# Sort pass of a graph network: VectorE's comparisons read the row of numbers from a PSUM bank

## The reference

```python
h = jnp.maximum(_layernorm(x, axis=-1), 0.0)
# layer 0, with row = src, col = dst
x_j = node_features[col]
m = jnp.einsum('ei,ej,ijh->eh', x_j, edge_attr_e3nn, W_msg_tp) * norm_msg_tp
m = jax.nn.silu(m)
m = m @ W_msg_lin * norm_lin
agg = jax.ops.segment_sum(m, row, num_segments=n_nodes)
...
x = x + layer0; x = x + layer1; x = x + layer2; x = x + layer3
```

## Time and profile before

| | |
|---|---|
| time, median of three runs | 19862.05 us (19857.42 to 19865.26) |
| the profiled execution | 19815.21 us, span 19813.6 us |
| instructions | 553,798 |
| PE busy over the whole span | 15287.0 us (77%) |
| DVE busy over the whole span | 13621.7 us (69%) |
| POOL busy over the whole span | 5755.4 us (29%) |
| stretch of the sort pass's scatters | 417.7 to 5958.6 us |

### The profile page before, as it was taken

How to read it: one execution, slowest core, us unless ns; L and a number is a source line. 1 busy time by engine, 2 the same in 40 slices (tenths; PEclk the granted TensorE clock), 3 DMA queues, 4 the chain that set the end, 5 groups by cost and what they waited for, 6 DMA issues and landing times. The chain is left out here.

```text
span 19813.6 us, 553798 instructions
## 1 busy us (share of the span) xinstructions
PE 15287.0 (77%) x200647; PEld 13589.7 (69%) x201524; DVE 13621.7 (69%) x32754; ACT 8118.3 (41%) x17256; POOL 5755.4 (29%) x4543
## 2 busy tenths in 40 slices
PE   2666666666666997799999999997688888856665
PEld 1666666666664996688888888886566666646565
DVE  3777777777775997555555555554677777769899
ACT  0444444444442332355555555553344444421111
POOL 1888888888880110011111111110000000001111
PEclk9555555555555997899999999998899999977676
DMA  2222222222222553344444444443344444427676
GB/s 56 54 54 50 53 54 54 54 52 52 54 51 66 157 157 91 91 110 110 110 110 108 112 109 111 108 111 80 114 139 139 140 142 139 139 61 210 173 209 181
DMA packets 1402755, 2062.56 MB, mean 104 GB/s; under 512 B 764952, under 2 KB 938022, under 8 KB 1359282
## 3 DMA queue, kind: packets, MB, share of 16 engines
q1 hardware_dynamic: 1089098, 1709.41, 27.8%
q0 software_dynamic: 218240, 197.29, 9.1%
q10 hardware_dynamic: 94544, 142.53, 2.0%
HBM read 1521.71 MB, written 523.16 MB: 103 GB/s over the span
## 5 line engine op out<-in xcount | busy, mean ns | idle before, releaser
L759 POOL DMA_INDIRECT records<-e_sort_rec,e_sort_index x3300 | 4328.5, 1312 | 1063.8 <-issue 989.5
L2442 POOL DMA_DIRECT2D states<-e_s_second_t x550 | 475.4, 864 | 4685.2 <-ACT e_s_second_t L2139 4342.2
L1088 PE MATMUL e_sort_acc<-e_sort_thirds,e_sort_hot 128*128 128x48 f32 x7260 | 1574.6, 414 | 320.8 <-DVE e_sort_hot L918 320.8
L1088 PEld LDWEIGHTS e_sort_acc<-e_sort_thirds,e_sort_hot 128*128 128x128 f32 x7260 | 1556.9, 332 | 353.2 <-DVE e_sort_hot L918 353.2
L2284 PE MATMUL e_s_ps_g<-e_s_parts,e_s_pick 128*128 128x64 bf16 x32670 | 1419.9, 198 | 276.0 <-DVE e_s_g_sb L1943 256.0
L2433 POOL DMA_INDIRECT e_s_spill<-send,e_s_lists x220 | 299.9, 1363 | 4257.3 <-PE e_s_ps_h L2344 3214.0
L2284 PEld LDWEIGHTS e_s_ps_g<-e_s_parts,e_s_pick 128*128 128x128 bf16 x32670 | 1301.5, 101 | 339.2 <-DVE e_s_g_sb L1943 290.8
L1943 DVE COPY e_s_g_sb<-e_s_ps_g 128x512 f32<-128x512 f32 x440 | 303.5, 690 | 1483.6 <-PE e_s_ps_h L2303 1376.5
L1926 DVE TENSOR_SCALAR e_s_pick<-e_s_rows,lane_below 128x1024 bf16<-128x1024 bf16 (+1 forms) x3300 | 1247.5, 436 | 3.2 <-PE e_s_ps_h L2326 3.1
L1005 ACT ACTIVATE e_sort_away<-iota,e_sort_slots 128x128 f32<-128x128 f32 x3850 | 1171.0, 388 | 10.7
L2354 PEld LDWEIGHTS e_s_ps_o<-w_eblk,e_s_act 128*128 128x128 f32 x7920 | 1040.8, 192 | 169.8 <-issue 146.5
(11 more groups left out here) (548 smaller groups left out, 37148.2 us busy)
## 6 DMA issues: line engine op xcount, KB each, us to landing
e_s_rows<-rows_d SPq DMA_DIRECT2D x330, 1088.0 KB, 5.3
e_s_hot<-hots_d SPq DMA_DIRECT2D x550, 560.0 KB, 3.9
e_s_to_rows<-rows_d SPq DMA_DIRECT2D x220, 608.0 KB, 5.4
e_s_rows<-rows_d SPq DMA_DIRECT2D x220, 544.0 KB, 4.1
e_s_rows<-rows_d SPq DMA_DIRECT2D x220, 512.0 KB
e_s_to_rows<-rows_d SPq DMA_DIRECT2D x220, 512.0 KB
states<-e_s_first_t ACTq DMA_DIRECT2D x440, 256.0 KB
states<-e_s_second_t POOLq DMA_DIRECT2D x440, 256.0 KB
```

The costliest lines, as they stand in the source:

```text
L759: pool.indirect_dma_start(records, bass.IndirectOffsetOnAxis(ap=index[x][:, t:t + 1], axis=0), rec[x][:, t, :], None,).then_inc(written[x] ...
L1088: mm = pe.matmul(acc[c // ACC][:, c % ACC * SPAN * F:(c % ACC + 1) * SPAN * F], hot[:, c, :], thirds[:, c, :, :].rearrange("p h f -> p (h ...
```

## The change

The row of numbers is also copied into PSUM, into columns 256 to 383 of `acc[3]` (`ps_iota`), once, after TensorE has blanked the four sum banks. The running sums are laid out anew: cells 0, 1 and 2 move into `acc[3]`, and the other thirty into `acc[0]` to `acc[2]`, ten each. The comparisons L818 and L823 and groups 0, 2 and 3 of L918 read the numbers from PSUM; group 1 of L918 goes on reading them from SBUF. TensorE signals a new step `early` when it has added cell 2, the last one that goes into `acc[3]`. VectorE waits for it ahead of group 2 of L918, and, for the block summed last, ahead of L818. In between, while group 1 is compared, TensorE may write `acc[3]`. The four final copies on ScalarE follow the new layout.

```diff
-            bt = Chain(sem(f"{name}_sum_t"), 0, ["rows"] + [f"added{g}" for g in range(len(HOTS))] + ["merged"])
+            bt = Chain(sem(f"{name}_sum_t"), 0, ["rows", "early"] + [f"added{g}" for g in range(len(HOTS))] + ["merged"])
...
+            ps_iota = acc[3][:, 256:256 + LANES]
+            blanked, iota_placed = sem(f"{name}_blanked"), sem(f"{name}_iota_placed")
+
+            def sum_bank(c):
+                return 3 if c < 3 else (c - 3) // ACC
+
+            def sum_at(c):
+                first = c if c < 3 else (c - 3) % ACC
+                return slice(first * SPAN * F, (first + 1) * SPAN * F)
...
                     dve.wait_ge(av.sem, av.at("cell", k))
+                    if before >= 4:
+                        dve.wait_ge(bt.sem, bt.at("early", k - 4))
                     dve.tensor_tensor(hot_c[:, :, :], bc3(cell[:, :], [P, BLOCK_T, SPILL]),
-                                      iota128[0:P, 0:SPILL].unsqueeze(1).broadcast_to([P, BLOCK_T, SPILL]), ALU.is_equal).then_inc(av.sem, 1)
+                                      ps_iota[0:P, 0:SPILL].unsqueeze(1).broadcast_to([P, BLOCK_T, SPILL]), ALU.is_equal).then_inc(av.sem, 1)
...
                         dve.tensor_tensor(hot_d[:, t:e, :], bc3(dlo[x][:, t:e], [P, e - t, LANES]),
-                                          iota128[0:P, :].unsqueeze(1).broadcast_to([P, e - t, LANES]), ALU.is_equal).then_inc(av.sem, 1)
+                                          ps_iota[0:P, :].unsqueeze(1).broadcast_to([P, e - t, LANES]), ALU.is_equal).then_inc(av.sem, 1)
...
                     for g, (c, e) in enumerate(HOTS):
+                        numbers = iota128[:, :] if g == 1 else ps_iota
+                        if g == 2:
+                            dve.wait_ge(bt.sem, bt.at("early", k))
                         dve.tensor_tensor(hot[:, c:e, :], bc3(lower[:, c:e], [LANES, e - c, LANES]),
-                                          iota128[:, :].unsqueeze(1).broadcast_to([LANES, e - c, LANES]), ALU.is_equal).then_inc(bv.sem, 1)
+                                          numbers.unsqueeze(1).broadcast_to([LANES, e - c, LANES]), ALU.is_equal).then_inc(bv.sem, 1)
...
                 dve.wait_ge(flushed, 7)
+                dve.wait_ge(blanked, 1)
+                dve.tensor_copy(ps_iota, iota128[:, :]).then_inc(iota_placed, 1)
+                dve.wait_ge(iota_placed, 1)
...
-                            mm = pe.matmul(acc[c // ACC][:, c % ACC * SPAN * F:(c % ACC + 1) * SPAN * F], hot[:, c, :],
+                            mm = pe.matmul(acc[sum_bank(c)][:, sum_at(c)], hot[:, c, :],
                                            thirds[:, c, :, :].rearrange("p h f -> p (h f)"), start=False,
-                                           stop=last and (c % ACC == ACC - 1 or c == OWN - 1), skip_group_check=True)
+                                           stop=last and (c == 2 or c % ACC == 2 and c > 2), skip_group_check=True)
+                            if c == 2:
+                                mm.then_inc(bt.sem, 1)
                         mm.then_inc(bt.sem, 1)
```

More of the change, by code:

```diff
@@ L1028, in _ @@
                 act.wait_ge(bt.sem, bt.end(BLOCKS - 1))
-                for b in range(4):
-                    act.activation(total[:, b * ACC * SPAN * F:min(CHUNKS, (b + 1) * ACC * SPAN) * F],
-                                   acc[b][:, 0:(min(CHUNKS, (b + 1) * ACC * SPAN) - b * ACC * SPAN) * F], ACT.Copy).then_inc(sums_flushed, 1)
+                for c in (0, 3, 3 + ACC, 3 + 2 * ACC):
+                    n = 3 if c == 0 else ACC
+                    act.activation(total[:, c * SPAN * F:(c + n) * SPAN * F], acc[sum_bank(c)][:, 0:n * SPAN * F], ACT.Copy).then_inc(sums_flushed, 1)
                 act.wait_ge(sums_flushed, 4)
@@ L1099, in _ @@
                 for b in range(4):
-                    pe.matmul(acc[b][:, :], blank[:, 0:LANES], blank[:, :], start=True, stop=False, skip_group_check=True)
+                    mm = pe.matmul(acc[b][:, :], blank[:, 0:LANES], blank[:, :], start=True, stop=False, skip_group_check=True)
+                mm.then_inc(blanked, 1)
                 def body(k, x, before):
```

## The result

The changed kernel took 19584.62 us in the median of 4 runs (19566.84 to 19610.17), the kernel before 19863.65 (19857.42 to 19886.99; three of its four runs are those of the table above): ratio 0.986, 95% interval 0.9845 to 0.9875. That is 279 us less, over four times the 64 that were forecast, and outside the range. The same two programs, run again in later batches, gave 0.9869 in one and 1.0008 in another. A batch is here a set of kernels run one after another on one chip, with the kernel before among them.

A forecast was written before the change was run, and what follows sets the result against it. POOL's scatters bound the kernel at 50.44 us a block, with TensorE's loop about 1 us shorter. 0.48 us x 108 = 52 us plus 12 us of lead make 64: 19862 - 64 = 19798 us, range 19700 to 19865.

The forecast's parts named there:

- The stretching: POOL's scatters L759, lengthened by VectorE comparisons with two SBUF operands: 2.46 us a block less, minus 0.5 kept by group 1.
- POOL's period, forecast at 48.5: POOL's time per block would fall by 1.96 us from 50.44 to 48.5 us; bounds of the fall 1.3 and 2.5.
- VectorE and the new wait: VectorE comparisons take no longer from PSUM; waiting for early before group 2 of L918 lasts 0.2 to 0.5 us, cost zero.
- The 65 ns: Skill-based estimate of extra time per VectorE instruction reading PSUM; would add 7 us in TensorE's loop; left out of the sum.
- That TensorE's loop becomes the bound: The loop of TensorE, ScalarE and VectorE, 49.5 us in the block shown, limits the block once POOL gets shorter.
- The sign that the prediction gave for being wrong: POOL's scatters still follow without a wait and the pass ends 200 us earlier; then TensorE's loop was elastic.
- What TensorE's loop gives back: Only its waits for VectorE's place stage: 0.24 us a block at L1044, 0.24 at L1067 (bounds 0 and 0.70); 52 us.
- The base of the sum: Period of 50.44 us a block before, falling to 49.96; the gain is taken off the median of 19862 us.
- POOL keeps the bound: Rival: TensorE's loop can follow down to 48.5 us, so all 1.96 us a block come off: 19646 us; chance 0.12.
- TensorE's loop is the bound already: Rival: the 0.48 us reappear as waits elsewhere in the loop; 19830 to 19862, say 19848 us; chance 0.20.
- the one slower case that I gave: Rival: TensorE's gathers L1067 lose their fast clock, 4.4 us in a block that loses it; 19919 us; chance 0.08.
- The lead of 12 us: Message values (L987) are ready 13 us before POOL takes them; this shrinks to nothing, so the last block starts 12 us earlier.

The follow-up runs named there:

- fourth batch: Changed kernel again 0.9869; kernel before with 14 of 30 scatters 0.9815; changed kernel with all four sum-stage comparison groups from PSUM 0.9841.
- third batch: Same programs again: kernel before 1.0004, changed kernel 1.0008, changed kernel with 28 of 30 scatters 0.9976, kernel before with 28 scatters 0.9949.
- a_place: Changed kernel, but the four sum-stage comparisons (L918) read the numbers from SBUF again, only the place stage from PSUM: 19740 us (0.9937).
- a_sum: Changed kernel, but the place-stage comparisons (L818, L823) read from SBUF again, without their wait; three sum-stage groups from PSUM: 19761 us (0.9946).
- b28: Kernel before with 28 instead of 30 scatters per block, two record columns left out: 19783 us (0.9944), again 19761 us (0.9949).
- Batches 1, 3 and 5: Batch 1: kernel before with 28 scatters 0.9944, with sorted records loaded a body later 0.9979; changed kernel with 28 scatters 0.9956, 32 scatters 1.0046.
- 2 and 4: Batch 2: 14 scatters in kernel before 0.981, in changed kernel 0.9815; changed kernel with only the place half 0.9937, only the sum half 0.9946.
- fifth: Kernel before again 1.0001; kernel before with 14 of 30 scatters 0.9836; changed kernel with all four sum-stage groups from PSUM 0.9944.
- b14: Kernel before with 14 instead of 30 scatters per block, 16 record columns not written: 19495 us (0.981), 19499 (0.9815), 19571 (0.9836).
- a_all: Changed kernel with group 1 of the sum stage from PSUM too, the wait moved ahead of it: 19551 us (0.9841), 19780 us (0.9944).

## Why the prediction was wrong

**The stretching: right.** Forecast were 2.46 us less 0.5 for group 1. Measured are 30 x (1312 - 1226) ns = 2.6 us in the result, 30 x (1312 - 1242) = 2.1 in the fourth batch and 30 x (1318 - 1255) = 1.9 in the third. POOL's period, forecast at 48.5, is 48.3 in the fourth batch, where POOL still paces (VectorE idles 6.5 us before `place`). Each half of the change took off its share. That comparisons with two operands in SBUF stretch the scatters stands against what the Trainium skill, page "SBUF — State Buffer", section "Who interferes with whom", infers from its probe: `tensor_tensor` takes only the read interface and the making of descriptors needs the write interface, so the one leaves the other alone. The same section's rule that a VectorE instruction with two SBUF inputs contends with a GpSimd instruction that reads SBUF is nearer to what these runs show: a_place and a_sum move only tensor_tensor operands, and the scatter mean goes from 1318 ns (before, third batch) to 1279 and 1282 over the whole pass, and to 1242 with both.

**VectorE and the new wait: right.** 1351 ns either way for the 1152 columns, 1218 for `hot_c` with PSUM against 1217 with SBUF; the wait takes 0.32 us a block against 0.2 to 0.5 forecast, and nobody is held up by it. The 65 ns that I had estimated from the Trainium skill, page "VectorE: DVE Perf Modes", section on the TRN2 errata, show in no row.

**That TensorE's loop becomes the bound: right** in the third batch, where POOL waits for L1005 in 85 blocks. In the result POOL stands level with it, and in the fourth batch POOL is the bound. The sign that the prediction gave for being wrong is what came: the scatters still follow each other without a wait, the last one starts 276 us earlier, and TensorE's loop was elastic.

**What TensorE's loop gives back: the step that failed.** The sum took 0.24 us at L1044 and 0.24 at L1067, from the waits of TensorE that the rows name, and held everything else in the loop fixed, on the ground that the matmuls are the same. The gather was not fixed. It was 11.96 us in the trace of before, and 9.9 us is what it takes undisturbed. Of the 2.1 us between, about 0.7 stood as TensorE's waits between its matmuls: these are the 0.70 us at L1067 in the earlier trace rows, of which the sum took 0.24 because "most stay". Next to nothing of them stayed in the result, where the line's idle time is 14.4 / 83 = 0.17 us a block and no product is named:

```profile
L1085 PE MATMUL e_sort_y<-e_sort_window,e_sort_turned 128*125 128x128 f32 x4996 | 756.4, 318 | 14.4 <-issue 10.7
```

Another 0.7 is in the matmuls themselves (774.8 / 79 = 9.8 us busy a block before, 756.4 / 83 = 9.1 after), which the prediction called the same, and 0.7 lies between the last matmul's end and the last product's (1.34 us before, 0.62 after). What I take for the cause of all three, products that start late, stood as waits of VectorE for TensorE, in two groups of 1000 to 5000 us of the kernel before that I hadn't weighed:

```profile
L885 DVE TENSOR_TENSOR e_sort_prod<-e_sort_y,e_sort_attr 125x512 f32<-125x512 f32 x553 | 377.9, 691 | 275.5 <-PE e_sort_y L1067 245.1 <-issue 23.3 <-remote 1.6
...
L885 DVE TENSOR_TENSOR e_sort_prod<-e_sort_y,e_sort_attr 125x256 f32<-125x256 f32 x79 | 33.5, 424 | 11.3 <-PE e_sort_y L1067 7.5
```

That is (275.5 + 11.3) / 79 = 3.6 us a block, where 1.8 is what TensorE's own pace leaves. The block of the earlier trace rows, a quick one, hardly showed it: its last 44 gathers take 5.91 us, those of a block of the result's trace 5.42.

**The base of the sum: the other half of the error.** The trace of before has late groups in a third, that of the result next to none. The time could not show it, since the kernel before takes the same time in both kinds: 19862 to 19867 beside the clean ones, 19862 to 19889 beside the late ones (it was never traced in a clean batch, so its short gather there is not shown). POOL paced it at 50.4 to 50.8 us, and the lateness hid in TensorE's slack. The change takes the cover away. Where groups are late, TensorE's loop of 50.7 us shows at once and the changed kernel gains 0; where they aren't, the loop is 47.8 us, and the time falls until POOL's 48.3 or TensorE's 47.8 stops it.

**The rivals.** In the clean batches and the result "POOL keeps the bound", 19646 us at 48.5 us a block, comes close (19585 and 19608; its 216 us are 1.96 us over 110 blocks, and over the forecast's 108 they would be 212). The reason I gave it only 0.12 was "no row of TensorE has 48.5", and that was the late trace's word. In the late batch "TensorE's loop is the bound already", 19848, is nearest (19879). The forecast of 19798 with 49.96 us a block is what b28 does in the late batches, 49.95 us and 19761 to 19783. That may be chance, since b28's loop comes to this length with other waits than the two of the sum. In the changed kernel the place stage came to lie beside other scatters, and its first turned tile is late there too (13.86 instead of 12.59 us to the gather), which ate the rest. The gathers kept their fast clock (the last 44 matmuls in 5.42 us in most blocks of the result); the one slower case that I gave didn't come.

**The lead of 12 us: right in the result** (from the 35th block on POOL's first scatter follows the end of L1005 by about 1.8 us; in the kernel before it is 12.0 in the mean), absent in the fourth batch, where POOL keeps a lag of 11.4.

**Not settled.** What makes a batch one of the late kind: it may be where the memory lies, or something else that stays for a batch. Batches 1, 3 and 5 and the trace of before had it; 2 and 4 hadn't. The chip alone is unlikely: the record numbers the chips 8, 10, 13, 1 and 1, so the fourth batch (clean) and the fifth (late) carry the same number, unless that number stands for different chips. Whether the result's batch was a clean one with exceptions, or one of the late kind in which the blocks mostly fell between the late places, is open too, so the rhythm isn't ruled out for that one trace. Nor which of the two is late, TensorE's matmuls or the signal at their end: the records start the next matmuls on time and say nothing of the end but the signal. Nor why some scatters do it and others don't: in the kernel before, with a third of the groups late, ScalarE's first turned tile was never late beside the 8th and 9th scatter of a block, while b14 in the fifth batch had it late in 101 of 102 blocks beside the 13th and 14th; and in the changed kernel of the third batch the first of the eight turned tiles is late in 91 blocks, the last six in none, though scatters run beside all eight. Scatters with fewer bytes, or in another place, weren't tried.

## What to carry to other kernels

A gain at the pace-setting engine is worth the slack of the next loop, and the slack is to be measured with the disturber gone (here: a kernel with 14 scatters, period 47.8), not read from waits in a trace in which it is present. Look at who waits for the engine of the next loop as well as at whom it waits for: 3.6 us a block before the products, with matmuls that needed half of that, was a loss inside the loop. And a result of 1% from one batch wants a second batch before it is believed: the same kernel gave 0.986, 0.987 and 1.001. The version that gained in either kind of batch is a_all, 0.984 and 0.994; in the fourth batch it ran beside the changed kernel and beat it, in the late kind the two never ran in one batch.

## What the runs showed of the hardware

In some batches TensorE's groups of matmuls are signalled late beside indirect DMAs of GpSimd, by up to 1.7 us (0.5 to 0.8 in the median of most traces), and then nearly always near one of two places of a scatter's 1.49 us, 0.75 apart; without scatters beside them 0 of 714 are late in each of four traces. The kind stays the same for all runs of a batch (10 runs of the changed kernel within 0.16% in the third). A VectorE wait of 1.6 us behind TensorE's first group of additions cost nothing, because the later groups had 3.9 us each.
